# A hybrid block (conv + state-space layer, attention, MLP) on one core: first scan ahead of the third softplus, next norm a row on, first loads and last norms rearranged, the MLP's residual added by TensorE

## The reference, cut to what matters

```
xn = rmsnorm(x, over channels) * w
u, z = in_proj(xn);  u = silu(causal_conv4(u) + b)       # and the same on the flipped sequence
dt, B, C = x_proj(u);  delta = softplus(dt_proj(dt) + b)
h[t] = exp(delta*A) * h[t-1] + delta*u*B                 # 16 states, 384 channels, both directions
y = sum over states (h*C) + u*D;  g = out_proj(y * silu(z)) * scale
x = x + res_scale * (g + sigmoid(depthwise3x3(xn)) * xn)
```

```
t = t + attention(layernorm(t));  t = t + proj(gelu(fc(layernorm(t))))   # fc, proj are Kronecker products, 1536 wide
```

## Time and profile before

| | us |
|---|---|
| median of 3 runs (4167.19 to 4175.09) | 4171.29 |
| the profiled execution, its own time | 4170.78 |
| its span, first to last instruction | 4169.0 |
| first scan of sample 0 | 111.78 |
| last scan of sample 7 | 3829.99 |
| VectorE busy | 3590.0 (86%) |
| TensorE busy | 3387.6 (81%) |
| POOL busy | 2760.9 (66%) |
| ScalarE busy | 2558.3 (61%) |
| mean granted TensorE clock | 0.879 of full |

### The profile page before, as it was taken

The page is one execution under the profiler, slowest core; times in us unless marked ns, Lnnn a source line. Parts: engine busy times, 40 slices in busy tenths (PEclk is TensorE's granted clock), DMA queues, the critical chain, the costliest instruction groups (busy, mean ns, idle before and its releaser), DMA issues.

```text
span 4169.0 us, 39529 instructions
## 1 busy us (share of the span) xinstructions
PE 3387.6 (81%) x11610; PEld 1710.0 (41%) x11626; DVE 3590.0 (86%) x2721; ACT 2558.3 (61%) x3547; POOL 2760.9 (66%) x1692
## 2 busy tenths in 40 slices
PE   6503499978898798978899798988999788976997
PEld 2201145623374245623365234732356233741472
DVE  4999998999899998999989998999989998997121
ACT  3533557665675767756676656757567656755362
POOL 2988786676766777676866767667876767675000
PEclk9756699989999799988999899987999889987998
DMA  2999797887878898888978978787978889788000
GB/s 82 229 238 232 191 236 173 213 198 197 216 184 197 197 217 193 193 201 200 230 169 208 212 190 213 184 195 200 233 173 210 196 202 214 171 207 188 6 7 15
DMA packets 220548, 772.36 MB, mean 185 GB/s; under 512 B 24908, under 2 KB 40574, under 8 KB 220062
## 3 DMA queue, kind: packets, MB, share of 16 engines
q0 software_dynamic: 114048, 415.29, 51.6%
q1 hardware_dynamic: 106270, 354.32, 25.8%
HBM read 339.60 MB, written 39.85 MB: 91 GB/s over the span
## 4 chain that ended last, share of the span: by engine, by line
PE 43%; DVE 23%; issue 14%; ACT 9%; POOL 7%; DMA 3%; SPq 0%; ACTq 0%; DVEq 0%; POOLq 0%
DVE pB L1205 15%; PE pW L674 9%; PE pW L591 9%; PE pW L479 7%; POOL hb L1388 5%; DMA y<-hb 3%; PE pW L556 3%; PE pW L607 2%; PE pW L522 2%; PE pW L570 2%; ACT pt L1008 2%; PE pW L534 2%; POOL prob L1369 2%; PE pW L649 1%; DVE hb L1214 1%
## 5 line engine op out<-in xcount | busy, mean ns | idle before, releaser
L1205 DVE TENSOR_TENSOR_SCAN pB<-pB,hb 128x1024 f32<-128x1024 f32 x768 | 1756.8, 2288 | 22.6 <-ACT pB L830 15.6
L1403 POOL DMA_DIRECT2D y<-hb x768 | 730.0, 950 | 753.4 <-DVE hb L1214 699.1
L1388 POOL TENSOR_TENSOR hb<-du_f,b_row 128x1024 f32<-128x1024 f32 x384 | 1003.9, 2615 | 177.9 <-DVE du_f L1154 131.3
L1388 POOL TENSOR_TENSOR hb<-uc_b,b_row 128x1024 f32<-128x1024 f32 x384 | 1002.7, 2618 | 73.8 <-DMA y<-hb 55.8
L1214 DVE TENSOR_TENSOR hb<-pB,c_row 128x1024 f32<-128x1024 f32 x768 | 940.0, 1224 | 45.4 <-DVE pB L1205 1.4
L830 ACT ACTIVATE pB<-delta,vec 128x1024 f32<-128x1024 f32 x384 | 429.0, 1117 | 321.1 <-DVE hb L1214 321.0
L830 ACT ACTIVATE pB<-xres,vec 128x1024 f32<-128x1024 f32 x384 | 428.8, 1118 | 295.5 <-DVE hb L1214 294.4
L674 PE MATMUL pW<-area,pt 128*128 128x64 f32 x3456 | 435.2, 280 | 20.1 <-ACT pt L1008 12.5
L674 PEld LDWEIGHTS pW<-area,pt 128*128 128x128 f32 x3456 | 407.6, 194 | 69.9 <-ACT pt L1008 59.8
L1249 DVE TENSOR_REDUCE stat<-pW 128x1 f32<-128x640 f32 (+7 forms) x361 | 258.6, 752 | 162.2 <-PE pW L594 162.2
L498 PE MATMUL pW<-area,xn_area 128*128 128x512 f32 x576 | 270.7, 625 | 49.4 <-DVE area L1292 36.1
(11 more groups left out here) (172 smaller groups left out, 4979.5 us busy)
## 6 DMA issues: line engine op xcount, KB each, us to landing
y<-hb POOLq DMA_DIRECT2D x768, 512.0 KB, 7.0
b_row<-bc_rows SPq DMA_DIRECT2D x256, 512.0 KB, 5.7
c_row<-bc_rows SPq DMA_DIRECT2D x256, 512.0 KB, 5.2
du_f<-in_x SPq DMA_DIRECT2D x8, 1536.0 KB, 13.1
kept_residual<-in_x SPq DMA_DIRECT2D x8, 1536.0 KB, 18.7
xres<-kept_residual SPq DMA_DIRECT2D x8, 1536.0 KB, 14.8
out_x<-xa SPq DMA_DIRECT2D x8, 1536.0 KB, 7.6
kept_residual<-hb POOLq DMA_DIRECT2D x16, 512.0 KB, 5.3
```

Of the source, the lines that this page charges most:

```text
L1205: dve.tensor_tensor_scan(flow(d, buf), flow(d, buf), flow(d, hb[r % NHB][:, :]), 0.0, ALU.mult, ALU.add).then_inc(scan_done, 1)
L1388: pool.tensor_tensor(hb[r % NHB][:, :], du[d][:, k, :], b_row[g % 2][:, :], ALU.mult)\
L1403: pool.dma_start(y[:, k, :], hb[r % NHB][:, :], accum_op=ALU.add).then_inc(y_in[k], 16)
```

## The change

The arithmetic is the same but for the place where the MLP's residual is added. The diff, cut to its core (the unchanged half of the moved blocks and the wrappers are left out):

```diff
-TAPS = (0, 3, 4, 6, 7, 9, 9)
+TAPS = (0, 3, 4, 6, 7, 8, 8)
...
-    + [("next_square", 0, S1 + 4), ("next_mean", 0, S1 + 4), ("next_rstd", 0, S1 + 5), ("next_norm", 0, S1 + 6)]
+    + [("next_square", 0, S1 + 4), ("next_mean", 0, S1 + 4), ("next_rstd", 0, S1 + 5), ("next_norm", 0, S1 + 7)]
-    + [("mlp_in", 0, S1 + 11), ("mlp_cast", 0, S1 + 12), ("mlp_split", 0, S1 + 13)] + mlp(0, S1 + 13) + ...
-SLOTS = [[(kind, n) for kind, n, row in STEPS + FINISH + PLAN + BEHIND if row == r] for r in range(ROWS)]
+    + [("mlp_in", 0, S1 + 11), ("mlp_cast", 0, S1 + 12), ("mlp_split", 0, S1 + 12),
+       ("mlp_low", 0, S1 + 13), ("mlp_fix", 0, S1 + 13)] + mlp(0, S1 + 13) + ...
+SOON = [x for x in BEHIND if x[0] == "step_abs"]
+SLOTS = [[(kind, n) for kind, n, row in STEPS + FINISH + SOON + PLAN + [x for x in BEHIND if x not in SOON] if row == r]
+         for r in range(ROWS)]
...
@@ sync: x first, seven constants (first_in), then w_in and the other eight (consts_in)
-            sp.dma_start(ip_w, w_in...).then_inc(win_in, 16)
             load_next(0)
...
+                sp.dma_start(dst, src).then_inc(first_in, 16)
+            sp.dma_start(ip_w, w_in...).then_inc(win_in, 16)
...
@@ tensor
+        def proj_bank(b, n):
+            return pW[:, (n + 2) % 4 if alone(b) else n % 2, :]
+        def proj_tile(n):
+            return (n % KT, n // KT) if n < 6 else ((n - 14) // 2, n % 2)
@@ out_project, ctx_t, wo, and finish and wo_add on vector
-                    m, c = t // 2, t % 2
+                    m, c = t % KT, t // KT
@@ ln_mean
-                            pe.wait_ge(wo_add, at(6, a, 6))
+                            pe.wait_ge(wo_add, at(6, a, 3 * c + 3))
@@ proj
-                    pe.wait_ge(ln_xn, at(4, a, 2))
+                    pe.wait_ge(ln_xn, at(4, a, 1 if n < (KT if alone(b) else 1) else 2))
@@ wo
-                    pe.wait_ge(ct_evac, at(6, a, 6))
-                    if n >= 4:
+                    if n < 4:
+                        pe.wait_ge(ct_evac, at(6, a, n + 3))
+                    else:
                         pe.wait_ge(wo_add, at(6, a, n - 3))
-                    project(pW[:, n % 4, :], o_w, ...)
+                    project(out_bank(n), o_w, ...)          # bank (n + 2) % 4
@@ mlp_in
-                    pe.wait_ge(ln_xn, at(4, a, 4))
                     for c in range(2):
+                        pe.wait_ge(ln_xn, at(4, a, 3 + c))
@@ mlp_out
+                    for m in range(KT):
+                        pe.matmul(pW[:, m, :], ident, xa[:, m, toks], start=True, stop=False)
                     pe.wait_ge(r_evac, at(2, a, n + 1))
                     for m in range(KT):
-                        mm = pe.matmul(pW[:, m, :], kout_w[...], rr[...], start=True, stop=True)
+                        mm = pe.matmul(pW[:, m, :], kout_w[...], rr[:, toks], start=False, stop=True)
@@ next_mean
-                    pe.wait_ge(wo_add, at(6, b - 1, 4))
+                    pe.wait_ge(wo_add, at(6, b - 1, 6))
@@ scalar
                 elif kind == "ln_rs" and not early:
-                    ... one Ln and one Exp over pS
+                    for bank, c in [(pW[:, 0, :], 1), (pW[:, 1, :], 2)] if alone(b) else [(pS, 2)]:
+                        ... Ln and Exp of this bank
+                elif kind == "mlp_low" and early:
+                    act.wait_ge(xr_step, at(5, a, 2))
+                    act.copy(xr_b, xr_rest[:, :]).then_inc(xr_step, 1)
+                elif kind == "mlp_add" and not early:
+                    act.wait_ge(fo_ready, at(2, a, n + 1))
+                    act.copy(xa[:, :, n * HALF:(n + 1) * HALF], pW[:, 0:3, :]).then_inc(x2_ready, 1)
...
-                    gates(b)
+                    tap_row_of(b, TAPS[6], 9)
+                    gates(b, 0, 2)
                     narrow_copies(b, 0)
+                    gates(b, 2, 3)
@@ vector: the hidden-weight split is now split_hidden(), called in sample 0 after both depthwise tiles;
@@         the small preparations are prepare(), called after the first norm (on all engines)
+                    dve.wait_ge(ln_rs, at(4, a, 2 * n + c + 1))
...
-                    dve.tensor_copy(xr_b, xr_rest[:, :]).then_inc(xr_step, 1)
-                elif kind == "mlp_add" and not early:
-                    ...
-                    dve.tensor_tensor(xa[:, :, toks], xa[:, :, toks], pW[:, 0:3, :], ALU.add).then_inc(x2_ready, 1)
...
-                    for k in range(KT):
+                    for k in range(2):
                         soft_sum(b, 0, k)
                         times_u(b, k)
...
                         scan_row(b, r, n, k, d)
                         output_row(b, r, n, k, d)
+                        if r == 0:
+                            soft_sum(b, 0, 2)
+                            times_u(b, 2)
```

More of the change, by code:

```diff
@@ L457, in _, with prepare @@
             sp.wait_ge(o_in, 16 * NB)
-        NCONST = 16 * 15
+        NFIRST, NCONST = 16 * 7, 16 * 8
         @block.tensor
         def _(pe):
-            pe.wait_ge(consts_in, NCONST)
-            rep = prob[0:12, C:2 * C]
-            for k in range(KT):
[L468 to L474, removed]
+            pe.wait_ge(first_in, NFIRST)
+            def prepare():
+                rep = pt[0:12, C:2 * C]
+                for k in range(KT):
+                    pe.matmul(pW[:, 0, k:k + 1], rep[:, 128 * k:128 * k + 128], small[0:12, 2:3], start=True, stop=True)
+                pe.matmul(pW[0:KI, 1, 0:C], small[0:12, 3:4].broadcast_to([12, KI]), rep, start=True, stop=True)
+                pe.wait_ge(prep_pool, 1)
+                pe.matmul(pW[:, 0, 8:10], small[0:1, 32:33].broadcast_to([1, 128]), small[0:1, 0:2],
+                          start=True, stop=True).then_inc(prep_pe, 1)
             def project(bank, w, cols, src, toks, done):
@@ L769, in iteration @@
                         step_size(b, 0, k)
+                    if isinstance(b, int) and b == 0:
+                        pe.wait_ge(fc_split, 5)
                     if layer1:
@@ L866, in silu_z, with gates @@
                     act.activation(zs[:, m, :], zs[:, m, :], ACT.Silu).then_inc(zs_ready, 1)
-            def gates(b):
-                for k in BRANCH:
+            def gates(b, lo, hi):
+                for k in BRANCH[lo:hi]:
                     if k < VK:
@@ L1071, in iteration @@
                             copy_u(0, t)
+                        act.wait_ge(prep_dve, 2)
                     for i in range(6):
@@ L1083, in iteration @@
                         soft_log(b, 0, k)
+                    if isinstance(b, int) and b == 0:
+                        act.wait_ge(fc_split, 5)
                     for k in range(2):
@@ L1121, in _ @@
-            dve.wait_ge(prep_pe, 1)
-            for k in range(KT):
-                dve.tensor_scalar(kin_w[:, k, :].rearrange("p (q i) -> p q i", q=4),
-                                  early[:, 160 + KI * k:192 + KI * k].unsqueeze(1).broadcast_to([128, 4, KI]),
-                                  pW[:, 0, k:k + 1], None, ALU.mult)
-            dve.tensor_tensor(kout_w, prob[0:KI, 0:C], pW[0:KI, 1, 0:C], ALU.mult)
-            dve.tensor_copy(small[:, 8:10], pW[:, 2, 0:2]).then_inc(prep_dve, 1)
@@ new lines, in prepare @@
+            def prepare():
+                dve.wait_ge(prep_act, 2)
+                dve.tensor_scalar(vec[:, :, V_A:V_A + NS], vec[:, :, V_A:V_A + NS], -1.0, None, ALU.mult)
+                dve.tensor_scalar(bq_s, vec[:, :, V_BQ], 0.125, None, ALU.mult)
+                dve.wait_ge(prep_pe, 1)
+                for k in range(KT):
+                    dve.tensor_scalar(kin_w[:, k, :].rearrange("p (q i) -> p q i", q=4),
+                                      early[:, 160 + KI * k:192 + KI * k].unsqueeze(1).broadcast_to([128, 4, KI]),
+                                      pW[:, 0, k:k + 1], None, ALU.mult)
+                dve.tensor_tensor(kout_w, pt[0:KI, 0:C], pW[0:KI, 1, 0:C], ALU.mult)
+                dve.tensor_copy(small[:, 8:10], pW[:, 0, 8:10]).then_inc(prep_dve, 1)
+                dve.wait_ge(prep_dve, 1)
+                dve.tensor_copy(rs_col, small[:, 9:10])
+                dve.tensor_tensor(g_col, small[:, 8:9], small[:, 9:10], ALU.mult).then_inc(prep_dve, 1)
+                dve.wait_ge(prep_dve, 2)
@@ L1269, in item @@
                     dve.tensor_tensor(xr_rest[:, :], pS, xr_a, ALU.subtract).then_inc(xr_step, 1)
-                    dve.wait_ge(xr_step, at(5, a, 2))
-                    dve.tensor_copy(xr_b, xr_rest[:, :]).then_inc(xr_step, 1)
+                elif kind == "mlp_fix" and not early:
                     dve.wait_ge(xr_step, at(5, a, 3))
```

110 lines of the change are left out of this document (56 added, 54 removed).

## The result

The changed kernel takes 4123.79 us (median of 4 runs, 4115.99 to 4132.68), the kernel before, run beside it, 4173.19 (4167.19 to 4176.18): a ratio of 0.9884, 95% interval 0.9861 to 0.9907. The forecast was 4102. The profiled execution took 4115.99, its span is 4114.2, so 54.8 us less than before by span, where the prediction had 69. This profiled execution is the shortest of the four, 7.8 us under their median, so rows read from it flatter the change a little. A row's number is that of its scan in the sample, counted from 0; row 5 is thus the time from scan 5 to scan 6.

What follows compares the result with a forecast made beforehand. VectorE, busy 86% of the span, was taken as the bound. From a median of 4171.3 us, the terms -23.5 - 1.6 + 1.4 - 22 - 27 + 34 - 20 - 3 - 7.6 = -69 gave 4102, range 4066 to 4140.

Steps and rivals of the forecast that it cites:

- the MLP split: MLP input's split: VectorE's bf16 cast goes to ScalarE, -2.9 us a sample, -20 in all (0 to -21).
- the next norm: Next sample's norm a row later, samples 1 to 6: scan 68 waits for its decay, +34 us (+24 to +44).
- the start up to the projection: Start of the run: squares wait for x alone, projection at 24.2 us instead of 47.8, -23.5 (-20.5 to -24).
- The rival that held the move free: Norm's move costs nothing, its extra wait being taken from later waits: 4068 us, chance 0.14.
- the one that halved the gain at the start: First constants land no sooner than the other loads, so the start gives half: 4114 us, chance 0.07.
- scan-ahead: Scan 0 ahead of the third softplus sum and product: -1.6 us in sample 0, part of -3.2 each between samples.
- the step sizes: Step-size rows, 14 times: abs and exp ahead of the projections' evacuations shorten VectorE's wait, -27 us (-29 to 0).
- The rival with these waits left in place: Step-size waits stay, because evacuations still preceding the logarithm come later with it: 4129 us, chance 0.13.
- between samples: Between two samples' rows, 7 times: earlier SiLUs and first logarithm, reordered scan 0, -3.2 us each, -22 in all.
- The MLP's residual: MLP residual, 14 times: TensorE identity products and ScalarE's copy replace VectorE's add, -3 us in all (-12 to +20).
- The rival of a late copy at low clock: TensorE at lower clock makes ScalarE's MLP copy late, scans 85 and 95 wait 6 us: 4183 us, chance 0.06.
- The tail: After the last row: projection starts after half a norm, less costs of table loads and identity products, -7.6 us (-13 to 0).

Runs made afterwards that it cites:

- Experiment 1: Two runs against the changed kernel: the split's rest kept in PSUM, 4098.36 us; the split as before, with VectorE's cast, 4126.8 us.
- experiment 3: Three runs undoing parts of the changed kernel: abs and exp behind evacuations, 4157.43 us; third sum and product ahead of row 0, 4121.4; old taps and gates, 4138.17.
- experiment 4: The changed kernel with VectorE adding the MLP's residual again, without identity products and ScalarE's copy: 4111.65 us, ratio 0.986.

## Why the forecast was right in direction and 22 us too low

**The step that failed is the MLP split.** The prediction took 2.9 us a sample for the cast and had no term for the subtraction behind it. The subtraction started 0.43 us ahead of POOL's product by the trace (844.51 and 844.94) and ended 1.09 us behind it (848.67 and 847.58), 4.16 us long against 1.21 in the tail. Experiment 1 shows both halves: without a second SBUF input 1.21 us and -20.6 in all; with the old split the same time as with the new. The distance of the starts doesn't tell who pays. In the next norm (sample 1, above) VectorE's first product, also with two SBUF inputs, starts 0.45 us ahead of POOL's and takes its 1.22; POOL's takes 2.95, and VectorE's second product is the one held, 3.36 us against 1.27 for the third. The split's subtraction, 0.43 us ahead, is held itself; both stand so in each of samples 1 to 6. Why the one and not the other is open. What the prediction should have done is to price both orders, 0 and -20: its bound of 0 was the outcome, its term of -20 was not.

**Right, and of its size:** the start up to the projection (24.52 for 24.2); the next norm, +33.5 for +34, by the named wait (scan 68, 5.64 us), and its undoing worth 36.9 at its place, sample 0 included. The rival that held the move free, and the one that halved the gain at the start, are out. Behind the projection the start leaked: without scan-ahead the first scan gains 22.7 and not 23.5; scan-ahead gives sample 0 0.6 at scan 1 and not 1.6; row 4 costs 2.4, which goes with the reordering (experiment 3), because POOL's product for row 5 comes late; and that sample's norm costs 2.7 and not 1.4.

**Right in kind, too small:** the step sizes, -39.3 for -27. The prediction left a wait of 1.4 to 1.7 us before the sum; in nine of fourteen there is none, in five 0.3 to 1.4, 4.6 us in all, and its ceiling of -29 (abs and exp whole) was too low. It priced ScalarE's order with TensorE's time held fixed. With abs and exp early, TensorE stood still for less long and made the second block's product at full clock, in 1.8 us less. By the rows with that product at half clock in the new order (experiment 3) this is worth about 1.6 us each, some 11 us of an excess of 12. That the clock held in all seven samples of this trace (1.00, once 0.82) is in part luck: after 2.8 us of idle time it was 0.50 in 11 of the 21 cases, 1.00 in eight and 0.79 or 0.82 in two. No run changes TensorE's idle time alone. The rival with these waits left in place is out.

**Right in sum, wrong in part:** between samples -19.7 for -22. The half credited to scan-ahead is there at scan 1 (10.6 us in samples 1 to 7), and 7 us of it are lost a few rows on, so that over the whole run undoing it changes nothing that can be told. What the prediction missed is a queue. It followed scan 1, and not what SP had in front of the B row of the third state. (Its SiLUs' end, 1447.2, is 1447.0 by its own terms; that changes nothing.)

**The MLP's residual**, -10.2 for -3: row 84's wait is 0.9 us as worked out (2.6 in sample 7), row 94's 2.65 instead of 1; rows 83 and 93 gain 2.6 us each time and not 1.7. No gain of the move itself is shown (experiment 4): VectorE's add is cheaper in the changed kernel than before, where it waited 12.6 us for TensorE in the fourteen rows, against 4.8 in experiment 4. The rival of a late copy at low clock, 6 us a time, is out at 0.9 and 2.65. **The tail**, -10.3 for -7.6, within its bounds. The prediction charged it 3.2 us for the identity products, and no run shows that price: without them the tail is no shorter. In it ln and exp of a half norm stand like this:

```profile
4035.66 0.66 ACT L995 ACTIVATE pW<-pW,tiny 128x512 f32<-128x512 f32 x1
4037.63 0.58 ACT L997 ACTIVATE pW<-pW 128x512 f32<-128x512 f32 x1
4040.05 7.11 PE L714 MATMUL pW<-area,kin_w 128*128 128x512 f32 x12 [2.81 <-DVE area L1283]
```

Ln ends at 4036.32 and exp starts at 4037.63, 1.31 apart, where the prediction put 1.28 for a table load.

So the total was 22 us off by the medians and 14 by the spans: +20 from the split, -12 from the step sizes, -10 from residual and tail, +8 from the start and the gaps, and +10 from small rows that no step had. That the time still fell inside the range is partly luck: with the 22 us that the step sizes, residual and tail gave beyond their terms taken away, it would be 4146, above the range's 4140.

## What to carry to other kernels

When an instruction that was held beside another engine's is removed, ask which one stands at that place next: here POOL's product stayed, and the next instruction with two SBUF inputs took 2.95 us more (4.16 for its 1.21), as much as the removed cast's whole 2.95. What helped was to take the second SBUF input away (a PSUM operand: 1.21 us), not the instruction. Of two pairs that started 0.43 and 0.45 us apart one went one way and one the other, so price both. And a row that is brought forward needs all of its inputs brought forward: read the issuing queue as well, for what stands in front of the load (4.45 us of POOL's wait in sample 1). An item may be moved past work that waits (abs and exp ahead of evacuations: 34 us by the medians for one line of order); it must not be moved in front of a decay that the next row needs (5.64 us before sample 1's scan 68).

## What the runs showed of the hardware

- A VectorE subtraction of 32x1024 with two SBUF inputs took 4.16 us beside a POOL product of 2.64 us that began 0.43 us later, in all seven samples; with one input from PSUM, at the same distance, 1.21 us.
- Three products of the norm, two SBUF inputs each, took 3.7 us with POOL idle (sample 0), 3.8 to 5.7 beside one POOL product (samples 1 to 6 of the changed kernel and of the run with the norm back) and 7.1 to 8.5 beside two (the run with rstd later).
- Which side is held was not to be told from the reported starts: a VectorE product 0.45 us ahead of POOL's ran in its 1.22 us and the next one was held, a subtraction 0.43 us ahead was held itself.
- The same four matrix products of TensorE, in samples 1 to 7 of all fourteen kernels, took 3.46 to 3.75 us behind 4.8 us of idle time (14 times, granted clock 0.50 to 0.54), 1.95 to 2.71 behind 1.1 to 1.3 (63 times, 0.70 to 1.00), and either 3.75 (11 times, 0.50) or 1.95 to 2.4 (10 times, 0.79 to 1.00) behind 2.8.
- A broadcast B row of 512 KB, issued just behind a load of weights, landed 8.3 to 10.0 us after its issue in the changed kernel and 4.7 to 6.8 us without scan-ahead, behind the same load; the page's median for such rows is 5.9.
